# Graph attention: one pass of vector operations for a pair of node blocks, and a tree of additions in place of a reduction over 41 slots

## The reference

```python
feat = (h @ W_gat).reshape(N, 4, 32)
e = leaky_relu(el[src] + er[dst], 0.2)          # one score per edge and head
ee = exp(e - segment_max(e, dst)[dst])
alpha = ee / segment_sum(ee, dst)[dst]
agg = segment_sum(feat[src] * alpha[:, :, None], dst)
r, z = sigmoid(i_r + h_r), sigmoid(i_z + h_z)   # gates from agg and from h
n = tanh(i_n + r * h_n)
x = x + elu((1 - z) * n + z * h)
```

## Time and profile before

| what | us |
|---|---|
| median of 3 timed runs | 11165.09 |
| lowest and highest of them | 11158.27, 11210.48 |
| span of the profiled execution | 12528.6 |
| attention stage in it, first gather to the end | 9801.5 to 12528.6 |
| VectorE busy in the whole span | 7716.2 |
| GpSimd busy in the whole span | 7476.5 |

### The profile page before, as it was taken

The page is one execution under the profiler, slowest core; times in us unless marked ns, Lnnn a source line. Parts: engine busy times, 40 slices in busy tenths (PEclk is TensorE's granted clock), DMA queues, the critical chain, the costliest instruction groups (busy, mean ns, idle before and its releaser), DMA issues. The chain is left out here.

```text
span 12528.6 us, 178083 instructions
## 1 busy us (share of the span) xinstructions
PE 6505.4 (52%) x38968; PEld 5397.9 (43%) x38968; DVE 7716.2 (62%) x17239; ACT 2933.1 (23%) x8407; POOL 7476.5 (60%) x7456
## 2 busy tenths in 40 slices
PE   3466666666475799999994444545555100000000
PEld 2355555555475677777764434434454100000000
DVE  9844444444498676666664444544576267777777
ACT  0011111111132344344432222322343000000001
POOL 5155555655200888888886888888800566666663
PEclk9966666666698999999997667766777555555555
DMA  1210000000733444444443333333322212221221
GB/s 41 65 36 2 2 2 2 2 2 2 14 41 50 93 93 94 92 94 95 92 93 49 50 51 53 54 50 52 54 42 34 35 49 50 51 50 48 51 54 40
DMA packets 1788557, 605.09 MB, mean 48 GB/s; under 512 B 1595943, under 2 KB 1729575, under 8 KB 1788260
## 3 DMA queue, kind: packets, MB, share of 16 engines
q1 hardware_dynamic: 1078132, 311.05, 12.8%
q0 software_dynamic: 255648, 274.30, 10.7%
q10 hardware_dynamic: 454736, 19.28, 3.0%
HBM read 430.75 MB, written 172.95 MB: 48 GB/s over the span
## 5 line engine op out<-in xcount | busy, mean ns | idle before, releaser
L1222 PE MATMUL c_acc<-c_spread_sb,c_basis_sb 128*125 128x256 f32 (+1 forms) x12544 | 2599.2, 376 | 1502.8 <-issue 655.0
L1222 PEld LDWEIGHTS c_acc<-c_spread_sb,c_basis_sb 128*125 128x125 f32 x12544 | 2266.5, 231 | 1803.5 <-issue 1536.3
L1614 POOL DMA_INDIRECT at_ring<-gat_table,at_place x1568 | 1585.7, 1011 | 1188.5 <-issue 1188.5
L609 POOL DMA_INDIRECT rec<-rk_rec,rk_place x1568 | 1619.3, 1033 | 1110.1 <-DVE rk_place L497 620.7
L1321 ACT ACTIVATE c_sums<-c_acc 125x512 f32<-125x512 f32 (+1 forms) x3136 | 1489.3, 490 | 2258.7 <-PE c_acc L1222 1298.6
L961 POOL DMA_INDIRECT c_ring<-hid_table,c_at x1568 | 1707.1, 1089 | 478.9 <-issue 443.2
L961 POOL DMA_INDIRECT c_ring<-feat_table,c_at x1568 | 1602.7, 1022 | 478.1 <-issue 462.9
L1084 DVE TENSOR_TENSOR c_spread_sb<-c_mark,c_rin 128x512 f32<-128x512 f32 (+1 forms) x3136 | 1745.2, 557 | 60.3
L1871 PE MATMUL gr_hps<-ident,gr_hs 128*32 128x128 f32 x98 | 29.8, 408 | 2473.7 <-issue 2066.3
L492 DVE CUSTOM_DVE_ANT_0 rk_junk_l<-rk_look_ps,rk_hi 128x98 bf16<-128x98 f32 x1568 | 402.2, 257 | 1324.1 <-remote 821.1
L1234 PE MATMUL c_mix<-c_sums,c_w 125*64 125x256 f32 (+1 forms) x9408 | 1037.3, 401 | 187.6 <-issue 133.8
(11 more groups left out here) (356 smaller groups left out, 10126.9 us busy)
## 6 DMA issues: line engine op xcount, KB each, us to landing
c_rin<-rows SPq DMA_DIRECT2D x3136, 42.0 KB
c_rin<-rows SPq DMA_DIRECT2D x3136, 20.0 KB
rows<-c_ring POOLq DMA_DIRECT2D x392, 128.0 KB
rows<-rk_blank SPq DMA_DIRECT2D x112, 252.0 KB
rows<-c_ring POOLq DMA_DIRECT2D x392, 72.0 KB
rows<-at_ring SPq DMA_DIRECT2D x196, 144.0 KB
rec<-rk_rec,rk_place POOLq DMA_INDIRECT x1568
c_ring<-hid_table,c_at POOLq DMA_INDIRECT x1568
```

Of the source, the lines that this page charges most:

```text
L609: pool.indirect_dma_start(out=d.rec, out_offset=bass.IndirectOffsetOnAxis(ap=place[:, u, j:j + 1], axis=0), in_=rec[:, u, j, :], in_offset ...
L1222: last = pe.matmul(acc[pp % BANKS][:, (w % 2) * WN * feats:(w % 2 + 1) * WN * feats], basis[:, q, w, :, :].rearrange("p a b -> p (a b)"), ...
L1614: pool.indirect_dma_start(out=ring[:, u, j, :], out_offset=None, in_=d.gat_table, in_offset=bass.IndirectOffsetOnAxis(ap=place[:, u, j:j + ...
```

## The change

The work on a pair is no longer done block by block. `body` makes mask, scores, peak, differences and the sum of weights for both blocks in one operation each, and ACT applies the exponential once for a pair. The eight products (four for each block, 1280 elements as before) follow one another, then `prod_made` is set once. The reduction over 41 slots is gone: slots are added in halves, 40 to 20 to 10 to 5 by additions of contiguous stretches, the old sum times its weight is put in as a sixth row, and 6 go to 3, 2 and 1; the last addition writes `c.acc` on VectorE. With that `sums` and the copy `take` on ACT fall away.

```diff
-                for v in range(2):
-                    pool.wait_ge(prod_made, (o * (NB // 2) + i) * 2 + v + 1)
-                    pool.sem_inc(pool_turn, 1)
+                pool.wait_ge(prod_made, o * HALF + i + 1)
+                pool.sem_inc(pool_turn, 1)
...
-                dve.tensor_scalar(out_of[:, v, :], slots[:, :], left[:, bass.ds(b, 1)], -BIG, ALU.is_ge, ALU.mult)\
-                    .then_inc(seq, 1)
+                dve.tensor_tensor(out_of[:, :, :], bc(slots[:, :].unsqueeze(1), [P, 2, RUN]),
+                                  bc(left[:, pair].unsqueeze(2), [P, 2, RUN]), ALU.is_ge).then_inc(seq, 1)
                 dve.tensor_tensor(s, el, er, ALU.add).then_inc(seq, 1)
...
+                for v in range(2):
+                    for k in range(4):
+                        w = slice(k * RUN // 4, (k + 1) * RUN // 4)
+                        last = dve.tensor_tensor(prod[:, v, w, :, :],
+                                                 bc(weight[:, v, w, :].unsqueeze(3), [P, RUN // 4, HEADS, FEAT]),
+                                                 bc(run[:, v, w, 0:FEAT].unsqueeze(2), [P, RUN // 4, HEADS, FEAT]), ALU.mult)
+                        if (v, k) != (1, 3):
+                            last.then_inc(seq, 1)
+                            after_step(8 + v * 4 + k)
+                last.then_inc(prod_made, 1)
+                dve.tensor_reduce(total[:, :, :], weight[:, :, 0:RUN, :].rearrange("p v s h -> p v h s"), X, ALU.add)\
...
-                dve.tensor_reduce(sums[:, v, :], prod[:, v, :, :, :].rearrange("p s h f -> p (h f) s"), X, ALU.add)\
-                    .then_inc(summed, 1)
+                def fold(out, x, y, n):
+                    dve.tensor_tensor(out, x, y, ALU.add).then_inc(folded, 1)
+                    dve.wait_ge(folded, item * folds + n)
...
+                for v in range(2):
+                    for w in (0, RUN // 4):
+                        n += 1
+                        fold(each[:, v, w:w + RUN // 4, :], each[:, v, w:w + RUN // 4, :],
+                             each[:, v, w + RUN // 2:w + 3 * RUN // 4, :], n)
+                after_step(16)
+                dve.tensor_tensor(den, den, total[:, :, :], ALU.add).then_inc(seq, 1)
+                for v in range(2):
+                    n += 1
+                    fold(each[:, v, 0:RUN // 4, :], each[:, v, 0:RUN // 4, :], each[:, v, RUN // 4:RUN // 2, :], n)
+                fifth = RUN // 8
+                n += 1
+                fold(each[:, :, 0:fifth, :], each[:, :, 0:fifth, :], each[:, :, fifth:2 * fifth, :], n)
+                dve.tensor_tensor(prod[:, :, fifth, :, :],
+                                  c.acc[:, pair, 0:P].rearrange("p b (h f) -> p b h f", h=HEADS),
+                                  bc(weight[:, :, RUN, :].unsqueeze(3), [P, 2, HEADS, FEAT]), ALU.mult).then_inc(seq, 1)
+                after_step(18)
+                third = (fifth + 1) // 2
+                for span in (third, 1):
+                    n += 1
+                    fold(each[:, :, 0:span, :], each[:, :, 0:span, :], each[:, :, span:2 * span, :], n)
+                dve.tensor_tensor(c.acc[:, pair, 0:P].unsqueeze(2), each[:, :, 0:1, :], each[:, :, 2:3, :], ALU.add)\
+                    .then_inc(acc_made, 1)
...
-            def take(b, item, v):
-                act.wait_ge(summed, item + 3)
-                act.activation(c.acc[:, bass.ds(b, 1), 0:P].rearrange("p b f -> p (b f)"), sums[:, v, :], ACT.Copy)\
-                    .then_inc(added, 1)
```

More of the change, by code:

```diff
@@ L1516, in attention_flow @@
                                                                           "exp_done"))
-    prod_made, summed, added = (sem(f"at_{x}") for x in ("prod_made", "summed", "added"))
+    prod_made, folded, acc_made = (sem(f"at_{x}") for x in ("prod_made", "folded", "acc_made"))
     pass_begun, stores_issued, dve_turn = (sem(f"at_{x}") for x in ("pass_begun", "stores_issued", "dve_turn"))
@@ L1524, in attention_flow @@
                                  "updated", "gate_seq", "out_stored"))
-    steps, gate_steps = 13, 7
+    steps, folds, gate_steps = 18, 9, 7
     H3 = 3 * FEAT
@@ L1542, in attention_flow @@
         weight = sb("at_weight", [P, 2, RUN + 1, HEADS])
-        prod = sb("at_prod", [P, 2, RUN + 1, HEADS, FEAT])
-        sums = sb("at_sums", [P, 2, P])
+        prod = sb("at_prod", [P, 2, RUN, HEADS, FEAT])
         wih, whh = sb("gr_wih", [H3, P]), sb("gr_whh", [H3, FEAT])
@@ L1672, in _ @@
             dve.tensor_copy(runs[:, :], runs_f[:, :]).then_inc(runs_ready, 1)
-            dve.sem_inc(prod_made, 2)
-            dve.sem_inc(summed, 2)
+            dve.sem_inc(prod_made, 1)
+            dve.sem_inc(acc_made, 1)
             dve.sem_inc(updated, 1)
@@ L1696, in scale @@
                 pair = bass.ds(i * 2, 2)
-                dve.wait_ge(added, item * 2 + (NB + 2))
+                dve.wait_ge(acc_made, item + 2)
                 dve.wait_ge(turned, item + 1)
@@ L1732, in gate, with body @@
                 dve.tensor_tensor(new, new, decay[:, :, :], ALU.add).then_inc(updated, 1)
-            def body(b, item, v):
+            def body(i, item):
                 def after_step(k):
                     dve.wait_ge(seq, item * steps + k)
[L1738 to L1741, removed]
-                dve.tensor_scalar(out_of[:, v, :], slots[:, :], left[:, bass.ds(b, 1)], -BIG, ALU.is_ge, ALU.mult)\
-                    .then_inc(seq, 1)
+                def fold(out, x, y, n):
+                    dve.tensor_tensor(out, x, y, ALU.add).then_inc(folded, 1)
+                    dve.wait_ge(folded, item * folds + n)
+                pair = bass.ds(i * 2, 2)
+                el = run[:, :, :, FEAT:GW]
+                er = bc(c.elr[:, pair, HEADS:2 * HEADS].unsqueeze(2), [P, 2, RUN, HEADS])
+                best = top[:, pair, :]
+                s = score[:, :, :, :]
+                dve.tensor_tensor(out_of[:, :, :], bc(slots[:, :].unsqueeze(1), [P, 2, RUN]),
+                                  bc(left[:, pair].unsqueeze(2), [P, 2, RUN]), ALU.is_ge).then_inc(seq, 1)
                 dve.tensor_tensor(s, el, er, ALU.add).then_inc(seq, 1)
                 after_step(2)
-                dve.tensor_tensor(s, s, bc(out_of[:, v, :].unsqueeze(2), [P, RUN, HEADS]), ALU.add).then_inc(seq, 1)
+                dve.scalar_tensor_tensor(s, bc(out_of[:, :, :].unsqueeze(3), [P, 2, RUN, HEADS]), -BIG, s, ALU.mult, ALU.add)\
+                    .then_inc(seq, 1)
                 after_step(3)
@@ L1749, in body @@
                 after_step(4)
-                dve.tensor_reduce(peak[:, v, :], s.rearrange("p s h -> p h s"), X, ALU.max).then_inc(seq, 1)
+                dve.tensor_reduce(peak[:, :, :], s.rearrange("p v s h -> p v h s"), X, ALU.max).then_inc(seq, 1)
                 after_step(5)
-                dve.tensor_tensor(peak[:, v, :], peak[:, v, :], best, ALU.max).then_inc(seq, 1)
+                dve.tensor_tensor(peak[:, :, :], peak[:, :, :], best, ALU.max).then_inc(seq, 1)
                 after_step(6)
-                dve.tensor_tensor(weight[:, v, 0:RUN, :], s, bc(peak[:, v, :].unsqueeze(1), [P, RUN, HEADS]),
+                dve.tensor_tensor(weight[:, :, 0:RUN, :], s, bc(peak[:, :, :].unsqueeze(2), [P, 2, RUN, HEADS]),
@@ L1755, in body @@
                                   ALU.subtract).then_inc(exp_ready, 1)
-                dve.tensor_tensor(weight[:, v, RUN, :], best, peak[:, v, :], ALU.subtract).then_inc(exp_ready, 1)
+                dve.tensor_tensor(weight[:, :, RUN, :], best, peak[:, :, :], ALU.subtract).then_inc(exp_ready, 1)
                 dve.wait_ge(exp_ready, item * 2 + 2)
-                dve.tensor_tensor(best, peak[:, v, :], peak[:, v, :], ALU.max).then_inc(seq, 1)
+                dve.tensor_tensor(best, peak[:, :, :], peak[:, :, :], ALU.max).then_inc(seq, 1)
@@ L1759, in body @@
                 dve.wait_ge(exp_done, item + 1)
-                dve.tensor_reduce(total[:, v, :], weight[:, v, 0:RUN, :].rearrange("p s h -> p h s"), X, ALU.add)\
-                    .then_inc(seq, 1)
[L1763 to L1779, removed]
@@ L1780, in body @@
-                last.then_inc(prod_made, 1)
-                dve.wait_ge(prod_made, item + 3)
-                dve.wait_ge(added, item + (NB - 1))
-                dve.tensor_reduce(sums[:, v, :], prod[:, v, :, :, :].rearrange("p s h f -> p (h f) s"), X, ALU.add)\
-                    .then_inc(summed, 1)
+                for v in range(2):
[7 more added lines that the diff above has]
+                            after_step(8 + v * 4 + k)
@@ new lines, in body @@
+                last.then_inc(prod_made, 1)
+                dve.tensor_reduce(total[:, :, :], weight[:, :, 0:RUN, :].rearrange("p v s h -> p v h s"), X, ALU.add)\
+                    .then_inc(seq, 1)
+                dve.wait_ge(prod_made, item + 2)
+                dve.wait_ge(acc_made, item + 1)
+                den = c.acc[:, pair, P:P + HEADS]
```

(25 more changed lines are left out.)

## The result

The changed kernel takes 11245.33 us (median of 4 runs, 11234.81 to 11264.07) against 11161.68 us for the kernel before (median of 4). The ratio is 1.0069, with a 95% interval of 1.0046 to 1.0092: slower by 83.7 us. The prediction was 11253 us.

A forecast was written before the change was run, and what follows sets the result against it. GpSimd's gather issues were taken to pace the attention loop at 46.3 us a pair. 46 x 2.3 = +106 us, less 18 at the end, gave net +88: 11253 us, 0.8% slower; range 10890 to 11320.

The forecast's parts named there:

- the slow register steps of the profiled execution: Attention loop, VectorE's sequencer: register steps of 0.70 us instead of 0.07, taken to belong mostly to the execution under the profiler.
- The rival with the slow steps: Attention loop: slow steps also in timed runs, so 53.2 us a pair before, 48.2 after; 10917 us, faster; chance 0.23.
- "the other stages" and "a somewhat faster GpSimd": Sources named for the rest of the profiled span's 1363 us excess, beyond the 317 us assigned to the attention loop.
- VectorE's sum: Attention loop: VectorE's own work for a pair falls from 41.5 to 34.0 us, a gain of 7.5 us.
- the rival with dear folds: Slot additions in halves (folds) cost 2.3 us each, each of seven gathers waits 0.8 us longer; 11510 us; chance 0.04.
- The "some 10 us": Attention loop: VectorE's expected idle time ahead of the copy to `run_at` in the profile after.
- What GpSimd pays: Attention loop: gathers slowed beside added two-operand operations cost GpSimd 1.5 to 3.2 us a step, taken as 2.3.
- the entry into a burst: Gathers falling in step with back-to-back VectorE operations: some 0.5 us extra, about 0.3 for the folds.
- the tree, 2.4 in the working: Seven more 1280-element additions in halves: 7 x 0.27 = 1.9, about 0.3 to fall in step, 0.2 for shorter folds.
- the merging, -0.5 in the working: Attention loop: one burst of eight products instead of two of four saves GpSimd 0.5 us a step.
- The end: After the last gather: two periods shrink by 7.5 us and the last pair by some 3, together -18 us.
- The rival that folds don't hold gathers: Attention loop: step stays 46.3 us, only the end's 18 us come back; 11147 us, or 11018 with fast issues; chance 0.09.

The follow-up runs named there:

- the additions against the reductions: Changed kernel with six more operations of 1280 elements for each pair behind the last fold: two-operand additions 1.0204, one-operand reductions 1.0107 of the kernel before.
- with products out of the way: Weights in PSUM, so products read one SBUF operand: changed kernel 11121 us; changed kernel with the tree undone, the strided reduction back, 10994 us.

## Why the prediction was right

**Which engine paces.** The step on which all hung was to set the slow register steps of the profiled execution aside. The second profile of before has none, on VectorE in its loop or in SyncE's stores, and a step of 46.12 us where the earlier trace rows had promised 46.3. The rival with the slow steps falls: its 53.2 us belong to one execution. Of its excess, 46 x (53.23 - 46.12) = 327 us lay in the loop and 1041 us ahead of the first run load, which came at 8880.18 and not at 9921.7. The working had left over what the loop did not explain for "the other stages" and "a somewhat faster GpSimd"; the second was not there. Why that execution was slow is not settled; no later profile shows it.

**VectorE's sum.** 34.0 us was forecast against 41.5; the runs with half the gathers measured 34.13 (34.55 between the rows shown) and 41.50. The fold at a product's price was right to a nanosecond or two (1.490 to 1.492), so the rival with dear folds falls too. For the time this sum decided only the end of the stage. The "some 10 us" of idle time ahead of the copy to `run_at` did not follow from it: 48.2 - 34.0 is 14.2, and 14.1 was measured.

**What GpSimd pays.** Forecast 2.3 us a step at an unknown issue pace, out of 1.5 to 3.2; measured 48.48 - 46.12 = 2.36. All of it lies in the length of the gathers: over the loop they took 1666.2 us and not 1558.0, which is 108.2 us more, while the idle time before them stayed at 448.7. The mechanism was right. That the size came out so close is in part luck: the pace turned out to be that of the trace, 0.95 + 0.30, and at that pace the working had given 1.9; the 2.3 allowed for a faster pace that no run showed.

The term that was too small is the entry into a burst. In all rows shown a gather that meets a burst ends 2.29 to 2.31 us behind the burst's start, some 0.8 us behind the end of its first operation. So the price is not fixed: the earlier in the burst a gather begins, the longer it lasts, 0.85 us too long for the 1.80 us gathers, 1.06 for the one of 2.01 and 0.42 for the one of 1.37. The working took 0.5 for the merging and 0.3 for the folds, although its own rows gave more: 3.8 - 8 x 0.27 leaves 1.64 for two bursts. And the folds stand in two bursts, since the small addition to the denominators parts them (the gather of 1.39 us at 10241.04). So the tree, 2.4 in the working, cost 3.12, and the merging, -0.5 in the working, gave -0.76; the two errors partly cancel.

**The end.** From the 47th run load to the end before took 153.8 us and after 132.1, so -21.7 where -18 was forecast. With 46 x 2.36 = 108.6 that makes +87; the medians differ by 83.7. The two profiled spans differ by 107.0: the other 20 us lie ahead of the first run load, in stages that the change leaves as they are.

**The rival that folds don't hold gathers** is refuted three times: by the 1.22 us beside folds, by the additions against the reductions, and by the tree's 3.0 us with products out of the way. Its time was also set too high by the working's own terms: even if folds held nothing, the merging would save an entry beside the products, and that step is 45.36 us, not 46.3. On the Trainium skill's page "SBUF — State Buffer", section "Who interferes with whom", an instruction of VectorE with two operands in SBUF contends with reads of GpSimd, and a reduction never contends. The runs agree with both (1.22 against 0.94 us, and 0.94 with one operand in PSUM); its remark that operations with two tensors were not seen to stall DMAs does not hold for these indirect gathers.

**The gain inside the change.** Taken alone the merging makes the kernel faster, 0.9963, since eight products in one burst cost one entry instead of two; the gathers' mean falls from 1058 to 1035 ns, which for 32 of them is 0.74 of the 0.76 us. The tree gives that back and more.

## What to carry to other kernels

Shortening an engine that waits is worth nothing, and how it is shortened may cost the engine that paces: here 17.8 us of one-operand reductions were free, and 12.9 us of two-operand additions were not. Price an operation by what runs beside it, not by its length alone. If GpSimd issues indirect DMAs, look for its issues stretching to the length of VectorE's operations; if they do, try one operand in PSUM, which here, with the merging and without the tree, took the kernel to 10994 us. When a profiled span does not agree with the timed runs, find the periods in the trace in which the other engine does not wait before believing the mean, and profile once more.

## What the runs showed of the hardware

A product of 1280 elements with one operand in PSUM took 1.491 us, no longer than the 1.492 with both in SBUF, and beside it gathers took 0.95 us instead of 1.22. Beside back-to-back operations of 1.49 us with two SBUF operands, one every 1.52 us, one gather came through for each (starts at 10223.68 and 10225.21), and the first ended 2.3 us behind the burst's start, however early it had begun. A reduction with a stride of 512 bytes took 1.70 ns an element (8.91 us for 5248), and a contiguous one 1.485 us for 1280, 1.16 ns each with its fixed cost.
